# First weight pieces, first root and last scatters of a transformer block at other places in the order

## The reference

```python
x = x + layernorm(attn(layernorm(x)))
x = x + layernorm(ffn(layernorm(x)))
# attn: qkv = x @ Wqkv.T + b; a = q k^T per head of 8 (no softmax); ctx = a v;
#       group norm of ctx per head over head channels and tokens, weight and bias; ctx @ out_w.T + out_b
# ffn:  shared silu(x Wg) * (x Wu) @ Wd over all tokens, plus the top 2 of 8 experts
#       per token by softmax(x @ gate_w.T), weights normalised to sum 1; hidden size 704
```

## Time and profile before

| | us |
|---|---|
| median of 3 runs | 841.98 |
| lowest, highest | 841.88, 842.23 |
| the profiled execution | 840.84 |
| its span in the trace | 839.1 |
| TensorE busy in it | 783.3 (93%) |
| VectorE busy | 588.7 (70%) |
| ScalarE busy | 487.4 (58%) |
| GpSimd busy | 277.0 (33%) |

### The profile page before, as it was taken

One profiled execution on the slowest core, in us unless ns is written; L12 is line 12 of the kernel. 1 busy time (PEld: TensorE's weight loads), 2 busy tenths in 40 slices (PEclk: granted clock), 3 DMA queues, 4 the chain that ended last, 5 costly groups with the idle time before them and its releaser, 6 DMA issues.

```text
span 839.1 us, 21195 instructions
## 1 busy us (share of the span) xinstructions
PE 783.3 (93%) x6686; PEld 642.8 (77%) x6695; DVE 588.7 (70%) x1568; ACT 487.4 (58%) x1073; POOL 277.0 (33%) x301
## 2 busy tenths in 40 slices
PE   6989999999999997778999999999999999999990
PEld 3547777777777776666888888888888888888880
DVE  5758989898989898897888644555555555555552
ACT  3364848484857576533466655565656565656561
POOL 3011010101010101002565555555555555555542
PEclk9999999999999999999999999999999999999996
DMA  4114444444444343203264567856464646464633
GB/s 194 51 36 172 113 145 114 145 122 153 119 148 129 132 115 130 45 14 90 53 171 77 98 70 72 123 96 131 76 152 72 148 69 151 74 147 68 147 39 94
DMA packets 102708, 90.11 MB, mean 107 GB/s; under 512 B 63776, under 2 KB 94240, under 8 KB 101472
## 3 DMA queue, kind: packets, MB, share of 16 engines
q1 hardware_dynamic: 87664, 68.45, 28.7%
q0 software_dynamic: 14976, 20.78, 17.5%
HBM read 48.70 MB, written 27.39 MB: 91 GB/s over the span
## 4 chain that ended last, share of the span: by engine, by line
PE 73%; DVE 15%; issue 5%; ACT 5%; POOL 1%; DMA 1%; ACTq 0%; DVEq 0%; POOLq 0%
PE ps L948 41%; PE ps L963 19%; PE ps L1067 4%; PE ps L1099 3%; DVE wgu L1355 3%; DVE hf L1295 2%; PE ps L1061 2%; ACT wgu L805 2%; DVE wdn L1355 1%; DVE st L1537 1%; DVE att L1462 1%; PE ps L1028 1%; DVE hT L1305 1%; DVE st L1275 1%; PE ps L1070 1%
## 5 line engine op out<-in xcount | busy, mean ns | idle before, releaser
L948 PE MATMUL ps<-xhl,wgu 128*128 128x256 f16 x3102 | 383.6, 273 | 7.0 <-DVE hf L1295 5.2
L948 PEld LDWEIGHTS ps<-xhl,wgu 128*128 (+1 forms) x3102 | 301.8, 98 | 50.4 <-DVE hf L1295 6.8
L1295 DVE SCALAR_TENSOR_TENSOR hf<-ps,sc,silu 128x256 f32<-128x256 f32 x330 | 159.7, 484 | 172.4 <-ACT silu L755 146.2
L963 PE MATMUL ps<-wdn,hT 128*128 (+1 forms) x1870 | 253.3, 273 | 11.3 <-DVE hT L1305 8.5
L755 ACT ACTIVATE silu<-ps,sc 128x256 f32<-128x256 f32 x275 | 130.0, 473 | 226.2 <-PE ps L948 223.0
L963 PEld LDWEIGHTS ps<-wdn,hT 128*128 128x128 f16 x1870 | 180.9, 98 | 38.0 <-DVE hT L1305 7.6
L696 POOL DMA_INDIRECT acc_d<-ysb,gst x78 | 128.6, 1649 | 44.5 <-POOL gst L692 30.9
L641 POOL TENSOR_TENSOR rstd<-ve,mhalf 128x4 f32<-128x4 f32 (+1 forms) x32 | 30.7, 959 | 294.2 <-DVE ve L1280 272.5
L769 ACT CAST hT<-hf 128x256 f16<-128x256 f32 x275 | 109.7, 399 | 12.1 <-DVE hf L1295 10.1
L1305 DVE TENSOR_TENSOR hT<-hf,hT 128x256 f16<-128x256 f32 x275 | 114.8, 417 | 1.7
L685 POOL DMA_INDIRECT attw<-xn_d,gst x74 | 75.9, 1025 | 42.1 <-POOL gst L681 30.9
(11 more groups left out here) (242 smaller groups left out, 775.3 us busy)
## 6 DMA issues: line engine op xcount, KB each, us to landing
wgu<-in_gu SPq DMA_DIRECT2D x8, 1408.0 KB, 6.2
att<-in_x SPq DMA_DIRECT2D x16, 512.0 KB, 5.6
wdn<-in_dn SPq DMA_DIRECT2D x8, 768.0 KB, 8.2
x_d<-att SPq DMA_DIRECT2D x8, 512.0 KB, 2.9
xn_d<-wgu SPq DMA_DIRECT2D x8, 512.0 KB, 3.4
acc_d<-ysb SPq DMA_DIRECT2D x16, 256.0 KB, 3.3
att<-x_d SPq DMA_DIRECT2D x8, 512.0 KB, 4.8
att<-acc_d SPq DMA_DIRECT2D x7, 512.0 KB
```

What stands on the lines that cost most here:

```text
L948: ins = te.matmul(o, slot_gu(slot, hw, k, j), x(hx, k), start=(n == 0), stop=(n == len(TERMS) - 1))
L963: ins = te.matmul(y_bank(u, tt), h(hh), slot_dn(slot, c, hw), start=(c == 0 and n == 0 and tt == 0), stop=(c == FC - 1 and n == 1 and tt = ...
L1295: v.scalar_tensor_tensor(out=hf[lo:P, c % 2 * TW:(c % 2 + 1) * TW], in0=up, scalar=scale_of(slot, 1, lo, P), in1=silu[lo:P, c % 2 * TW:(c ...
```

## The change

Three things are moved or left out. In `START`, the step `prep` of batch 0 is taken apart into `prep_hi` (ScalarE's high half) and `prep_lo` (VectorE's low half), which stand at places of their own; `x2` stands ahead of the key and value steps, the fourth piece is no longer behind `logits`, and one of two `busy` products behind the first statistics is gone. In the first stage the root stands between the two affine selects, and GpSimd waits for the normalisation before the second select; `weight_hi` and `weight_lo` of the first 256 columns stand behind the halves of the turned x. The last three tiles' scatters, which are written out behind the loop, read their index columns where they lie.

```diff
-START = [(-1, "busy", 9), (-1, "ln1_stats"), (-1, "busy", 2), (-1, "ln1_apply"), (-1, "turn1"), ...
+START = [(-1, "busy", 9), (-1, "ln1_stats"), (-1, "busy", 1), (-1, "ln1_apply"), (-1, "turn1"), ...
...
@@ make_pick
                 pool.wait_ge(pick_link, 2)
+                root(LN1, 0, NT)
+                pool.wait_ge(xn_made, 1)
                 g.affine_select(out=pick_f, in_=pick_f, compare_op=ALU.is_ge, fill=0.0, base=2,
...
                     if b < 0:
                         make_pick()
-                    root(LN1, b + 1, NT)
+                    else:
+                        root(LN1, b + 1, NT)
...
-            def scatter(i):
-
+            def scatter(i, last=False):
+
+                rows = idx_s[:, i * TT:(i + 1) * TT] if last else idxc[:, 4:6]
                 pool.wait_ge(y_made, (2 * B + i + 3) * TT)
                 wait(pool, scattered, 16 * TT * i)
-                g.tensor_copy(idxc[:, 4:6], idx_s[:, bass.ds(i * TT, TT)]).then_inc(idxs_made, 1)
-                pool.wait_ge(idxs_made, i + 1)
-                passed(pool)
+                if not last:
+                    g.tensor_copy(rows, idx_s[:, bass.ds(i * TT, TT)]).then_inc(idxs_made, 1)
+                    pool.wait_ge(idxs_made, i + 1)
+                    passed(pool)
...
             for i in range(NTILE - 3, NTILE):
-                scatter(i)
+                scatter(i, last=True)
...
@@ scalar
-            act.wait_ge(wscale_made, 1)
-            weight_hi(0, D)
...
                     if b < 0:
+                        act.wait_ge(wscale_made, 1)
+                        weight_hi(0, D)
                         weight_hi(D, 3 * D)
...
-                if kind == "prep":
+                if kind in ("prep", "prep_hi"):
                     prep(b, step[1], stg_gu, stg_dn)
...
@@ vector
                     if b < 0:
                         weight_scale()
-                        weight_lo(0, 0, D)
...
                     if b < 0:
+                        weight_lo(0, 0, D)
                         weight_lo(1, D, 3 * D)
...
-                if kind == "prep":
+                if kind in ("prep", "prep_lo"):
                     prep(b, step[1], stg_gu, stg_dn)
```

More of the change, by code:

```diff
@@ L48 @@
          ("D", 10), ("prep", 3), ("D", 11), ("logits",), ("logits_out",)]
-START = [(-1, "busy", 9), (-1, "ln1_stats"), (-1, "busy", 2), (-1, "ln1_apply"), (-1, "turn1"), (-1, "busy", 8), (-1, "turn1_out"), (-1, "q"), (-1, "q_out"), (-1, "kv", 0),
+START = [(-1, "busy", 9), (-1, "ln1_stats"), (-1, "busy", 1), (-1, "ln1_apply"), (-1, "turn1"), (-1, "busy", 8), (-1, "turn1_out"), (-1, "q"), (-1, "q_out"), (-1, "kv", 0),
          (-1, "kv_out", 0), (0, "prep_max", 0), (-1, "kv", 1), (0, "prep_max", 1), (-1, "kv_out", 1), (-1, "kv", 2), (0, "prep_max", 2),
@@ L52 @@
          (0, "ctx_out"), (0, "prep_spread"), (0, "channel_stats"), (0, "busy", 9), (0, "ln1_stats"), (0, "group_mean"), (0, "busy", 9), (0, "group_var"),
-         (0, "busy", 8), (0, "ln1_apply"), (0, "turn1"), (0, "ctx_norm"), (0, "prep_scale"), (0, "turn1_out"), (0, "prep", 0), (0, "prep", 1), (0, "out"),
-         (0, "lno_stats"), (0, "q"), (0, "prep", 2), (0, "lno_apply"), (0, "q_out"), (0, "busy", 10), (0, "kv", 0), (0, "kv_out", 0), (0, "kv", 1),
-         (0, "kv_out", 1), (0, "kv", 2), (0, "kv_out", 2), (0, "x2"), (0, "ln2_apply"), (0, "kv", 3), (0, "turn2"), (0, "kv_out", 3),
-         (0, "state"), (0, "xhl"), (0, "state_out"), (0, "rows2"), (0, "logits"), (0, "prep", 3), (0, "logits_out")]
+         (0, "busy", 8), (0, "ln1_apply"), (0, "turn1"), (0, "ctx_norm"), (0, "prep_scale"), (0, "turn1_out"), (0, "out"), (0, "prep_hi", 0),
+         (0, "lno_stats"), (0, "prep_lo", 0), (0, "prep_hi", 1), (0, "prep_hi", 2), (0, "q"), (0, "lno_apply"), (0, "prep_lo", 1), (0, "q_out"), (0, "busy", 10),
+         (0, "x2"), (0, "kv", 0), (0, "kv_out", 0), (0, "kv", 1), (0, "kv_out", 1), (0, "prep_hi", 3), (0, "kv", 2), (0, "kv_out", 2),
+         (0, "ln2_apply"), (0, "prep_lo", 2), (0, "prep_lo", 3), (0, "kv", 3), (0, "turn2"), (0, "kv_out", 3),
+         (0, "state"), (0, "xhl"), (0, "state_out"), (0, "rows2"), (0, "logits"), (0, "logits_out")]
 PE_FIRST, PE_SECOND = tuple(range(B)), (0, B - 1)
@@ L686, in gather_x @@
                                          bass.IndirectOffsetOnAxis(ap=rows[:, t:t + 1], axis=0)).then_inc(xg_loaded[r], 16)
-            def scatter(i):
+            def scatter(i, last=False):
+                rows = idx_s[:, i * TT:(i + 1) * TT] if last else idxc[:, 4:6]
                 pool.wait_ge(y_made, (2 * B + i + 3) * TT)
                 wait(pool, scattered, 16 * TT * i)
-                g.tensor_copy(idxc[:, 4:6], idx_s[:, bass.ds(i * TT, TT)]).then_inc(idxs_made, 1)
-                pool.wait_ge(idxs_made, i + 1)
-                passed(pool)
+                if not last:
+                    g.tensor_copy(rows, idx_s[:, bass.ds(i * TT, TT)]).then_inc(idxs_made, 1)
+                    pool.wait_ge(idxs_made, i + 1)
+                    passed(pool)
                 for t in range(TT):
-                    g.indirect_dma_start(acc_d, bass.IndirectOffsetOnAxis(ap=idxc[:, 4 + t:5 + t], axis=0), ysb[:, t * D:(t + 1) * D], None,
+                    g.indirect_dma_start(acc_d, bass.IndirectOffsetOnAxis(ap=rows[:, t:t + 1], axis=0), ysb[:, t * D:(t + 1) * D], None,
                                          compute_op=ALU.add).then_inc(scattered, 16)
```

## The result

The changed kernel took 837.09 us, the median of 4 runs (836.78 to 837.86), beside 842.11 (4 runs, 841.88 to 842.43) for the kernel before on the same chip. The ratio is 0.9941, with a 95% interval of 0.9924 to 0.9959. So it is 5.0 us faster where the prediction said 3.2, and it lies 0.2 us under the lower end of the range. The profiled execution took 836.78, span 835.0, against 840.84 and 839.1 before: 4.1 between these two.

A forecast was written before the change was run, and what follows sets the result against it. TensorE was taken to bound the long middle, a ladder of small waits the first 63 us, and an uncovered chain the end. Terms -2.05 - 0.5 - 0.65 = -3.2 us from median 841.98 gave 838.8; range 837.3 to 840.4.

The forecast's parts named there:

- The middle's 2.05: Second stage, 40 to 63 us: moved weight pieces start out statistics earlier, root still held by piece 0's low half; -2.05 us.
- Rival C: Second stage: root of the out rows not held by piece 0's low half; 0.9 us more gain, 837.9; chance 0.06.
- Rival B: Middle's gain lost because something counted as following holds the first expert product; only 0.5 + 0.65 remain, 840.8; chance 0.13.
- taking away the low half alone would give 0.02 us: Ahead of the first expert product: context product ends at 62.27, last low half at 62.29, so both must come earlier.
- The start's 0.5: First stage: earlier root and reordered weight halves gain 0.5 us, though select and cast each hold one scale instruction; bounds 0 to 1.6.
- Rival A: First stage: the scale's tiny instructions are not held, so the start gives 1.1 instead of 0.5; 838.2; chance 0.22.
- The rule of the Trainium skill that spoke against this move: First stage: two-port copies, casts and tensor_scalar exclude GpSimd; the second issued is blocked until the first is done.
- The tail's 0.65: Last tile's scatter: without the index copy it is issued 0.31 us behind the last y row instead of 0.96; -0.65 us.
- Rival D: Start: TensorE's clock low over 17.70:24.90, products 5.4 us later against 3.2 gained, 844.2; chance 0.04.
- The detour over the profiled execution: Forecast time: 3.2 us off the profiled 840.84 gives 837.6; the runs' median lies 1.14 above, hence 838.8.
- TensorE is the engine of the long middle, and the change touches nothing there: Long middle: nothing changes except one small row of work before each of the last three scatters.

The follow-up runs named there:

- e10: Changed kernel with piece 0's low half behind the shift, piece 1's behind the second shift, 6 instead of 10 keep-busy products: 836.37 us, ratio 0.9926.
- e8: Changed kernel with GpSimd waiting for the scale instead of the normalisation before the second select: 838.16 us, ratio 0.9945.
- e9: Kernel before with only the root between the selects, weight halves still ahead of x's: 842.8 us, ratio 1.000.
- e13: Changed kernel repeated without edit on a third, slower chip: 840.87 us beside 845.9 for the kernel before, ratio 0.9944.
- e1: Kernel before repeated without edit: 842.23 us, ratio 1.000.
- e5: Changed kernel repeated without edit: 838.58 us beside 843.14 for the kernel before, ratio 0.9953.
- e11: Changed kernel with GpSimd waiting for the scale before the second select and the root free of piece 0's low half: 835.86 us, ratio 0.9915.
- e12: Changed kernel with the index-column copies put back before the last three scatters: 839.31 us, ratio 0.9956.
- e6: Kernel before with 20 instead of 10 keep-busy products behind q, filling TensorE's pause: 843.0 us, ratio 1.0002.
- e7: Changed kernel without the 10 keep-busy products behind q, opening TensorE's pause: 839.66 us, ratio 0.9962.

## Why the prediction was right in its mechanisms and wrong in its size

Two steps failed. The sum of the moved waits was too small: 3.2 where the marks give 3.6, and more than half of the lack is the last low half, put at 0.02 us where it gave 0.24. And the forecast took this sum for the whole difference, with the long middle untouched; the means differ by 4.4 to 4.9, and the 0.8 to 1.3 us that no mark of the change gives are the larger part of the miss.

**The middle's 2.05** came out as 2.04, with the root held as forecast: it ends 0.86 us after the low half. Rival C is refuted for this kernel, and what it said is true of another: without the low half beside the root 1.4 us more come, where I had put at most 0.9 above. That bound was worked out for a low half that stays ahead of the shift; e10 puts it behind, which I had not considered. Rival B did not happen: everything down to the context product moved by the same amount.

**"taking away the low half alone would give 0.02 us"** is the first step that failed. I compared the low half's end (62.29) with the end of the context product by its row, 60.29 + 1.98 = 62.27. In the kernels where nothing else is in the way the next product starts 1.82 us after the context product's start (changed kernel, e10). So TensorE would have been free at 62.11, and in before it waited for the low half: the row of the weight load at 62.34 names VectorE as what ended its wait, and 62.35 - 62.11 = 0.24 us is what the move of this piece gave on top. The end of a product is modelled, and I took a difference of 0.02 us from it. That the last low half would then be clear of the way was right: it ends at 51.92 + 1.94 = 53.86, 5.65 us ahead of the first expert product.

**The start's 0.5** was 0.57, by the very path forecast: two tiny instructions held until the select's and the cast's ends, the scale at 12.09 for the forecast 12.0. Rival A is refuted in the changed kernel; e8 shows that its 1.1 was there to be had (0.57 + 0.64 = 1.21). "Gain 0.5" hangs on the other move, as forecast: without it e9's bias turn is 0.31 late. The rule of the Trainium skill that spoke against this move ("SBUF — State Buffer", section "Who interferes with whom") agrees with the 0.74 and 0.67 us here, and e8 shows it from the other side, in GpSimd's casts.

**The tail's 0.65** was 0.75: 1.86 - 1.11. The forecast counted 0.31 us from the copy's start; the scatter comes 0.27 us behind the end of the y rows (818.08 + 0.84 = 818.92, 819.19), which ends a little ahead of where the copy stood.

**Rival D**, the clock as a loss at the start, did not happen. In none of the traces was the clock low in 17.7 to 24.9. The low level ahead of it is no property of either kernel: in e13, the changed one, the turns take 1.97 us where they take 1.09 at full clock, and the bias turn comes at 17.19 as without it.

**The sum by these corrected terms is 3.6**, which would have given 838.4, and a median of 837.1 was measured. The detour over the profiled execution ("The median of the runs is 841.98, 1.14 above it") is not to blame: it cancels, since the forecast is nothing but 841.98 - 3.2, and before's median beside the changed kernel was 842.11. The second step that failed is "TensorE is the engine of the long middle, and the change touches nothing there": everything between the first expert product and the last scatter was put at no difference. The medians hold what happens there too. Its time differs between executions, first of all by the fall of the clock near 334 us, 1.66 us or nothing, and in the traces the changed middle met this fall less often. Nor is TensorE without waits there: in 325 to 376 us of the profiled execution of before it was busy for 36.57 of 51.00 us.

**What stays open** is 0.8 to 1.3 us: the mean differences are 4.4 and 4.9, the marks 3.6; with each mean known to 1.1 or 1.2 us, a part of it may be scatter alone. Two observations bear on it.

The first is the fall near 334 us: 7 of 8 traces against 4 of 9, at 1.66 us each, would be 0.7 us of difference in the mean (an estimate from few traces). The fall behind the pause of 2.46 us, in 2 of the 6 traces that have the old middle with its pause, at 1.43 us each, would be 0.5 more, but filling that pause did not give it back.

The second observation is each run's mean granted clock. In the 31 runs of before beside e1 the time falls by 0.37 us for each 0.001 of clock (correlation -0.64), and the changed kernel's runs have more clock: 0.9846 and 0.9838 (e5, e13) for 0.9821 and 0.9820 of before beside them. That is 1.8 to 2.5 thousandths, or 0.7 to 0.9 us by that slope, about what is missing. The slope is not the same on each chip, though: among before's 23 runs beside e13 it is 0.34, but among the 18 beside e5 only 0.07 (correlation -0.09), by which e5's clock would be worth 0.2. The other kernels with the new middle have it too (e10 0.9838, e11 0.9848, e12 0.9832 for 0.9816), and their mean differences also exceed their marks, by about 0.9 to 1.5 us. Against it: over 14 experiments this surplus and the gain in clock go together only with a correlation of 0.6, and e6 and e7 have 1.8 thousandths more clock each and no surplus (-0.4 and -0.3).

So that the surplus is less time at 1.2 GHz is likely and not shown. The place near 334 us is the best candidate; why a middle that runs 2 to 3 us earlier should meet the fall less often there, or whether it does, the runs do not say. What would settle it is both kernels with TensorE kept busy ahead of that place, or many more traces of each. The 0.4 us between scatter and final statistics may be another part of it.

## What to carry to other kernels

Keep long VectorE instructions with two SBUF inputs out of the place between a statistic and the GpSimd root that follows it, and keep GpSimd's selects and casts away from a serial chain of tiny VectorE instructions: each such pair cost 0.6 to 1.4 us at the next mark here, and moving one of the two by a step got that back. An order changed for one such reason can create the other (e9). And work out a difference between two kernels from fixed marks of both traces, and look for a mark whose distance takes two values over traces of one program: that is where the medians can differ by more than the marks of the change. One profiled execution can lie some 2 us from another of its kernel by chance, and a distance read to a modelled end of a product is no better than a quarter of a microsecond.

## What the runs showed of the hardware

- A GpSimd root of 128x4 (1.01 to 1.05 us alone) lasts 1.71 us beside a VectorE instruction of 1.01 us with two SBUF inputs and 2.37 beside one of 1.68, and ends 0.86 to 0.87 us after it each time.
- A 128x2 VectorE tensor_scalar of 0.17 us lasts 0.74 or 0.67 when it is issued beside a GpSimd select or cast, and just one in each: the chain pays the rest of the GpSimd instruction, not a price per instruction.
- The same kernel, alike to 0.01 us up to 334 us, had the TensorE clock at 2.4 GHz in one execution and at 1.2 GHz in the other behind the same stretch of part-time work (5.43 busy of 9.00 us). That fall cost 1.66 or 1.67 us in each of the 11 traces of 17 that have it. Behind a pause of 2.46 to 2.6 us it fell in two traces, for 1.43 us, and did not in five.
